# One change to a two-layer transformer kernel: modulation of layer 2 after the linear attention, q and k stored feature-major with three-run gathers, first row maxima ahead of second-half stores

## What is computed

```python
# layer 1, first half: linear attention, 16 heads of 16, rope, elu+1, chunks of 64
# layer 1, second half: gelu MLP, 2048 wide, 4-bit weights with block scales
# layer 2, first half: causal softmax attention, 16 heads of 16, with rope and biases
# layer 2, second half: RMS norm, causal softmax attention without rope,
#                       RMS norm, SwiGLU-like MLP 1024 wide with a low-rank term
x = x + gate * block(layernorm(x) * (1 + scale) + shift)     # each half
att = softmax(q @ k.T / 4, causal) @ v                       # the two softmax attentions
```

## Time and profile before

| what | us |
|---|---|
| median of 3 runs | 708.69 (708.49 to 711.36) |
| profiled execution | 708.0 |
| its span, first to last instruction | 706.1 |
| PE busy | 654.3 (93%) |
| DVE busy | 457.2 (65%) |
| ACT busy | 334.4 (47%) |
| POOL busy | 149.7 (21%) |
| mean granted TensorE clock | 0.988 of full |

### The profile page before, as it was taken

How to read it: one execution, slowest core, us unless ns; L and a number is a source line. 1 busy time by engine, 2 the same in 40 slices (tenths; PEclk the granted TensorE clock), 3 DMA queues, 4 the chain that set the end, 5 groups by cost and what they waited for, 6 DMA issues and landing times.

```text
span 706.1 us, 10697 instructions
## 1 busy us (share of the span) xinstructions
PE 654.3 (93%) x3990; PEld 405.8 (57%) x3990; DVE 457.2 (65%) x970; ACT 334.4 (47%) x531; POOL 149.7 (21%) x194
## 2 busy tenths in 40 slices
PE   4999979999999879899999998897999999999996
PEld 3667647777777656455444434483554444368884
DVE  5668787777777388778888602557788886242223
ACT  5334243333333423345567684561564657843332
POOL 3002224555555601310000000031100001003331
PEclk9999799999999999999999999999999999999999
DMA  7602410000000002663000000037410000050001
GB/s 263 227 0 91 128 44 0 24 23 22 1 0 1 0 1 75 190 186 92 2 2 2 1 2 1 1 125 227 137 54 2 2 2 2 20 160 1 1 0 59
DMA packets 36415, 38.34 MB, mean 54 GB/s; under 512 B 4034, under 2 KB 35292, under 8 KB 36108
## 3 DMA queue, kind: packets, MB, share of 16 engines
q1 hardware_dynamic: 36364, 37.67, 17.0%
HBM read 30.11 MB, written 7.34 MB: 53 GB/s over the span
## 4 chain that ended last, share of the span: by engine, by line
PE 47%; issue 22%; POOL 12%; DVE 11%; ACT 3%; DMA 2%; SPq 2%; POOLq 0%; DVEq 0%; ACTq 0%
POOL it_lo L1602 9%; PE psum L782 9%; PE psum L742 8%; PE psum L768 8%; PE psum L454 4%; DVE m L1285 3%; PE psum L455 3%; PE psum L456 3%; POOL wd L1581 2%; PE psum L771 2%; PE psum L745 2%; PE psum L471 2%; PE psum L570 1%; DVE mx L1285 1%; SPq L345 1%
## 5 line engine op out<-in xcount | busy, mean ns | idle before, releaser
L962 ACT ACTIVATE pt<-psum 128x1024 f32<-128x1024 f32 (+1 forms) x192 | 148.1, 811 | 93.2 <-PE psum L771 65.1
L1285 DVE TENSOR_REDUCE mx<-psum 128x1 f32<-128x512 f32 (+3 forms) x216 | 132.4, 665 | 16.3 <-PE psum L742 8.3
L742 PE MATMUL psum<-kr,qr 96*128 96x512 bf16 (+3 forms) x384 | 108.6, 332 | 5.7 <-DVE m L1285 2.7
L768 PE MATMUL psum<-qr,kr 99*128 99x512 bf16 (+3 forms) x384 | 97.6, 327 | 1.5 <-ACT pt L962 1.3
L1602 POOL TENSOR_TENSOR it_lo<-it,it_hi 128x512 fp32r<-128x512 f32 x48 | 67.3, 1402 | 146.2 <-ACT it_hi L1006 144.6
L782 PE MATMUL psum<-pt,vp 128*32 128x512 f32 (+3 forms) x768 | 81.7, 498 | 0.0
L454 PE MATMUL psum<-h_hi,wf_hi 128*128 128x512 f32 x192 | 75.4, 393 | 1.7 <-issue 1.7
L742 PEld LDWEIGHTS psum<-kr,qr 96*128 96x128 bf16 x384 | 36.3, 98 | 68.0 <-DVE mx L1285 29.4
L1006 ACT CAST it_hi<-it 128x512 fp32r<-128x512 f32 x48 | 29.9, 623 | 95.7 <-DVE it L1360 95.7
L455 PE MATMUL psum<-h_lo,wf_hi 128*128 128x512 f32 x192 | 74.8, 390 | 0.0
L456 PE MATMUL psum<-h_hi,wf_lo 128*128 128x512 f32 x192 | 74.8, 389 | 0.0
(11 more groups left out here) (201 smaller groups left out, 1087.1 us busy)
## 6 DMA issues: line engine op xcount, KB each, us to landing
qr<-parts_scratch SPq DMA_DIRECT2D x48, 128.0 KB, 2.7
kr<-parts_scratch SPq DMA_DIRECT2D x48, 128.0 KB, 2.6
parts_scratch<-parts SPq DMA_DIRECT2D x12, 384.0 KB, 3.2
wmod<-in_L_wmod SPq DMA_DIRECT2D x1, 1536.0 KB, 6.3
parts_scratch<-qr SPq DMA_DIRECT2D x4, 384.0 KB, 3.2
x<-in_L_attn_x SPq DMA_DIRECT2D x2, 512.0 KB, 4.3
wmod<-in_L_wmod SPq DMA_DIRECT2D x1, 1024.0 KB, 5.3
packed<-in_L_ffn_gate_W_packed SPq DMA_DIRECT2D x1, 1024.0 KB, 7.2
```

The lines of the kernel that those rows point to most:

```text
L742: m = pe.matmul(b, qr[0:PARTS_ROWS, c, h, (qt - 4 * c) * P:(qt - 4 * c + 1) * P], kr[0:PARTS_ROWS, ch, h, 0:w], start=True, stop=not diag)
L768: m = pe.matmul(bank[4 + 2 * at[0] + j][:, 0:w], kr[0:PARTS_ROWS + 3, kt // 4, h, (kt % 4) * P:(kt % 4 + 1) * P], qr[0:PARTS_ROWS + 3, c, ...
L962: act.activation(pt[:, n % 4, :, 0:w], psum[:, b:b + 2, 0:w], ACT.Exp, scale=0.25).then_inc(S["ex"], 1)
L1285: dve.tensor_reduce(dst, bank[at[0]][:, 0:k * w].rearrange("p (k w) -> p k w", k=k), AX, ALU.max).then_inc(S["p1_mx"], 1)
```

## The change

It does these things: (1) `wmod1` gets bytes beside `wmod0` and is loaded as soon as layer 1's weights are converted; its twelve calls move behind `update(0)`, eight ahead of layer norm 1's transposes and four behind, each with one filler matmul in front, in place of the fillers of 20 and 8. In the linear attention three fillers per tile stand in their place from tile 1 on. The copy on DVE moves behind `halves(1)`, and PE waits for it ahead of the MLP. (2) The memset of `vp` is cut in four, behind `it_lo` of units 4 to 7 (and behind the scaling in the odd ones). (3) The rows of q and k are reordered to (feature, head) by permuting weights and biases on the host; the pieces are ordered low, middle, high for k and high, middle, low for q, so that one `spread` is 6 DMAs, of 384, 256 and 128 KB for q and for k, each gated by its own store. The order in which the six products are summed changes with it. (4) `row_max(l, 0)` goes ahead of `parts_out(l, 1, 0)` on SP. (5) The six fillers ahead of each attention's first score go.

```diff
-        (wmod0, raw0), (wmod1,), (scale,), (parts, vp), (b_hi, m_hi) = overlay(
+        (wmod0, raw0), (_, wmod1), (scale,), (parts, vp), (b_hi, m_hi) = overlay(
...
-            [("wmod1", [P, KC, 1536], F32)],
+            [("wmod0_", [P, KC, 1536], F32), ("wmod1", [P, KC, 1536], F32)],
...
-        scr = nc.dram_tensor("parts_scratch", [4, P, 3, T], BF16, kind="Internal").ap()
+        scr = nc.dram_tensor("parts_scratch", [4, 3, P, T], BF16, kind="Internal").ap()
...
-            sp.wait_ge(S["mod_mm"], 2)
+            sp.wait_ge(S["wt_hi"], 5)
+            sp.wait_ge(S["wt_lo"], 4)
             load(wmod1[:, :, :], a["L1_wmod"].rearrange("(c p) n -> p c n", p=P), "ld_wmod1")
...
-            sp.wait_ge(S["mod_mm"], 3)
+            sp.wait_ge(S["mod_mm"], 2)
             for j in range(FC[0] // 2):
...
-                    sp.dma_start(scr[w2, :, :, tok], piece(l, w2, half)).then_inc(S[f"pw{2 * half + dt}"], 16)
+                    sp.dma_start(scr[w2, :, :, tok].rearrange("s p t -> p s t"), piece(l, w2, half)).then_inc(S[f"{'qk'[is_k]}w{2 * half + dt}"], 16)
...
-                sp.wait_ge(S[f"pw{2 * half + dt}"], 32 * (l + 1))
-                for is_k, (dst, order) in enumerate([(qr, (0, 1, 0, 1, 0, 2)), (kr, (1, 1, 2, 2, 0, 1))]):
-                    for slot, part in enumerate(order):
-                        sp.dma_start(dst[slot:PARTS_ROWS:6, half, 8 * dt:8 * dt + 8, :],
-                                     scr[2 * dt + is_k, :, part, tok].rearrange("(h d) t -> d h t", d=DH)
+                for is_k, dst in enumerate((qr, kr)):
+                    sp.wait_ge(S[f"{'qk'[is_k]}w{2 * half + dt}"], 16 * (l + 1))
+                    for first, part, n in ((0, 0, 3), (3, is_k, 2), (5, 2 * is_k, 1)):
+                        src = scr[2 * dt + is_k, part:part + n].rearrange("s (d h) t -> (s d) h t", d=DH)
+                        sp.dma_start(dst[DH * first:DH * (first + n), half, 8 * dt:8 * dt + 8, :], src[:, :, tok]
                                      ).then_inc(S[f"qr_ld{2 * half + dt}"], 16)
...
                 spread(l, 0, 1)
+                row_max(l, 0)
                 parts_out(l, 1, 0)
-                row_max(l, 0)
                 parts_out(l, 1, 1)
...
             for t in range(NT):
-                if t >= 2:
-
-                    if t == 2:
-                        pe.wait_ge(S["ld_wmod1"], 16)
-                    modulation(wmod1, 1, 7, 2 * t - 4)
-                    m = modulation(wmod1, 1, 7, 2 * t - 3)
-                    if t == 7:
-                        m.then_inc(S["mod_mm"], 1)
+                if t >= 1:
+                    idle(3, 7)
...
             pe.wait_ge(S["q_e"], 8)
-            pe.wait_ge(S["mod_cp"], 3)
             attention_transposes(0)
...
-            idle(20, 4)
+            pe.wait_ge(S["ld_wmod1"], 16)
+            for j in range(8):
+                idle(1, 4)
+                modulation(wmod1, 1, 5, j)
             layer_norm(1)
-            idle(8, 4)
+            for j in range(8, 12):
+                idle(1, 4)
+                m = modulation(wmod1, 1, 5, j)
+            m.then_inc(S["mod_mm"], 1)
             pe.wait_ge(S["ln_f"], 8)
             pe.wait_ge(S["ln_hl"], 8)
+            pe.wait_ge(S["mod_cp"], 3)
             mlp(0)
...
-                            pe.wait_ge(S[f"qr_ld{2 * c + g // 2}"], 16 * 12 * (l + 1))
+                            pe.wait_ge(S[f"qr_ld{2 * c + g // 2}"], 16 * 6 * (l + 1))
...
                             if blk == 0:
-                                idle(6, 4)
                                 pe.wait_ge(S["kr_ones"], 4)
...
-            modulation_copy(2, 1, 7, 0, 12)
             modulation_rest(0)
...
             halves(1)
+            modulation_copy(2, 1, 5, 0, 12)
             modulation_rest(1)
...
-                    pool.memset(vp[:, :, :, :], 1.0).then_inc(S["vp_ones"], 1)
...
                     if n % 2 == 1 and f == 0 and n // 2 + 2 < FC[f]:
                         scaled(n // 2 + 2)
+                    if f == 0 and 4 <= n < 8:
+                        if n == 4:
+                            pool.wait_ge(S["mod_mm"], 3)
+                        pool.memset(vp[:, 2 * n - 8:2 * n - 6, :, :], 1.0).then_inc(S["vp_ones"], 1)
+                        pool.wait_ge(S["vp_ones"], n - 3)
...
+    spread = _np.arange(D).reshape(2, 8, DH).transpose(0, 2, 1).reshape(-1)
+    for n in ("L1_attn_Wq", "L1_attn_Wk", "L1_ffn_Wq", "L1_ffn_Wk"):
+        given[n] = _np.ascontiguousarray(given[n][:, spread])
```

More of the change, by code:

```diff
@@ L326, in build @@
             att_t at_e wo_m ysem bt x_upd
-            qt sp_h sp_r sp_m sp_l sp_p pw0 pw1 pw2 pw3 qr_ld0 qr_ld1 qr_ld2 qr_ld3 vp_e
+            qt sp_h sp_r sp_m sp_l sp_p qr_ld0 qr_ld1 qr_ld2 qr_ld3 vp_e
             p1_s p1_mx m_max m_step m_t m_c m_ld0 m_ld1 s2 ex pv ob ot at_r
@@ L331, in build @@
             dq w_sc wf_h wf_l g_m u_m gl_s it_s it_h it_l fdn out_done""".split()
+        names += [f"{z}w{i}" for z in "qk" for i in range(4)]
         names += [f"nat{i}" for i in range(FC[1])] + [f"ld_scale{i}" for i in range(4)]
@@ L926, in middle @@
                     half, n = divmod(w, 4)
-                    act.copy(piece(l, n, half)[:, (1, 2)[n % 2], :], rest[:, w % 4, :]
+                    act.copy(piece(l, n, half)[:, 1, :], rest[:, w % 4, :]
                              ).then_inc(S["sp_m"], 1)
@@ L935, in split @@
                             for i in range(4):
-                                act.wait_ge(S[f"pw{i}"], 32)
-                        act.copy(piece(l, n, half)[:, (0, 1)[n % 2], :], bank[w % 4][:, :]
+                                act.wait_ge(S[f"qw{i}"], 16)
+                                act.wait_ge(S[f"kw{i}"], 16)
+                        act.copy(piece(l, n, half)[:, (0, 2)[n % 2], :], bank[w % 4][:, :]
                                  ).then_inc(S["sp_h"], 1)
@@ L1182, in rope_cos @@
                     dve.wait_ge(S["rp_add"], 8 * l + t - 1)
-                dve.tensor_tensor(t1[:, t % 2, :].rearrange("p (h d) -> p h d", d=DH),
-                                  bank[4 + 2 * (t % 2)][:, :].rearrange("p (h d) -> p h d", d=DH),
-                                  rope_c[:, l, t, :].unsqueeze(1).to_broadcast([P, 2 * H, DH]), ALU.mult
-                                  ).then_inc(S["rp_t1"], 1)
+                if l == 0:
+                    z = [v.rearrange("p (h d) -> p h d", d=DH) for v in (t1[:, t % 2, :], bank[4 + 2 * (t % 2)][:, :])]
+                    c = rope_c[:, l, t, :].unsqueeze(1).to_broadcast([P, 2 * H, DH])
+                else:
+                    z = [v.rearrange("p (g d h) -> p g d h", g=4, h=8) for v in (t1[:, t % 2, :], bank[4 + 2 * (t % 2)][:, :])]
+                    c = rope_c[:, l, t, :].unsqueeze(1).unsqueeze(3).to_broadcast([P, 4, DH, 8])
+                dve.tensor_tensor(z[0], z[1], c, ALU.mult).then_inc(S["rp_t1"], 1)
             def rope_sin(l, t):
@@ L1691 @@
             inputs[n].reshape(FC[1], P, KC, P).transpose(0, 3, 2, 1).reshape(F1, D))
[L1692 to L1693 removed]
+    spread = _np.arange(D).reshape(2, 8, DH).transpose(0, 2, 1).reshape(-1)
+    for n in ("L1_attn_Wq", "L1_attn_Wk", "L1_ffn_Wq", "L1_ffn_Wk"):
+        given[n] = _np.ascontiguousarray(given[n][:, spread])
+    given["bias_rows"] = _np.concatenate(
+        [_np.array(inputs[n]) for n in ("L0_attn_bq", "L0_attn_bk", "L0_attn_bv", "L0_attn_bg")]
+        + [_np.array(inputs[n])[spread] for n in ("L1_attn_bq", "L1_attn_bk")])
     for name, arr in [*given.items(), ("rope_cos", cos), ("rope_sin", sin)]:
```

31 lines of the change are left out of this document (16 added, 15 removed).

## The result

The changed kernel takes 719.7 us (median of 4 runs, 717.6 to 722.2); the kernel before took 708.9 beside it. The ratio is 1.0134, 95% interval 1.0104 to 1.0164. It is slower, by 10.8 us by the medians and 9.5 us by the ratio, where 706.2 us, 2.5 us faster, was forecast. The profiled execution took 719.4 us, its span 717.5, against 706.1.

A forecast was written before the change was run, and what follows sets the result against it. PE's waits with DVE close behind bound linear attention, a PE-independent POOL/ACT/DVE loop the MLP, DVE the attention starts; -1.0 + 0.2 + 2.2 - 1.6 - 2.3 = -2.5 us gave 706.2 on the 708.69 median, range 702.5 to 711.5.

The forecast's parts named there:

- Linear attention, -1.0: Linear attention: fillers replace modulation pairs, DVE then limits, w_lo and the add to x come 1.0 us earlier; bounds 0.4, 2.0.
- The clock of 1.00 from 70 to 78 us: Sign in the linear attention: denser fillers keep TensorE at full clock there, with the last w_lo about 1 us earlier.
- Around layer norm 1, +0.2: Behind update 0: the twelve calls hide under DVE's chain; only DVE's 0.16 us copy with its hand-over adds, +0.2 us.
- rival B: Modulation stretch behind update 0: the clock falls there, kernel slower, 708 to 713 us, middle 711; chance 0.22.
- over 6.0: Condition for the clock-fall rival behind update 0: it decides once the eight calls take more than 6.0 us; 5.7 expected.
- Memset, +2.2: MLP loop: odd-unit memsets make it_lo collide with wf_lo, about 1.1 us each; even ones cost 0; bounds 0 and +4.0.
- First attention, -1.6: First attention, ahead of the first score: the six fillers' 1.81 us go, 1.6 us kept because scores may run at half clock.
- gathers half as many in number come earlier than needed and give nothing: First attention: fewer gathers give no gain, since PE reaches the first bank by the splits; 0 us.
- Second attention, -2.3: Second attention: earlier gathers shorten PE's waits, and removed fillers give 1.3 us; sum -2.3, bounds -0.5 and -3.5.
- Half the issues ... bring `qr_ld0` some 4 us forward: Second attention, SP: at 0.74 us per issue, fewer gathers let PE start 0.4 to 0.5 us before 478.14.
- rival D: Gathers: 384 KB pieces land later than three of 128, DMA engines limit, second attention starts as before; 707 us, chance 0.04.
- Rival C: Both attentions: without fillers first scores run longer at half clock, gaining 0.5 each instead of 3.9 together; 709.1 us, chance 0.08.

The follow-up runs named there:

- the repeated change: The changed kernel unaltered, measured again beside its two halves and against the kernel before: 721.7 us, ratio 1.0148.
- the one-column pattern: Gathers half alone, rows two apart, its 28 fillers behind update 0 replaced by 12 fillers, each with two unread one-column matmuls: 708.4 us, repeated 710.7.
- The run with six calls in the gap: Changed kernel with six spaced gather pieces and even-unit memsets; six modulation calls in PE's wait in update 0, then 20 fillers, six calls after layer norm: 710.3 us.
- the second comparison: The gathers half alone with rows two apart, modulation and memset as before, measured again against the kernel before: 707.8 us, ratio 0.9925.

## Why the prediction was wrong

**Linear attention, -1.0.** Right in mechanism, and a little large. From the first `kv_pair` matmul to the add to x, nine profiled executions with the modulation in its old place took 33.6 to 34.1 us in seven cases and 36.9 in two; nine with it moved took 32.7 to 34.0, medians 33.8 and 33.4: 0.4 us, and no execution with the long case. The clock of 1.00 from 70 to 78 us did not come in the first execution: it was 0.84 in 72 to 76 and 0.73 in 76 to 80. Over all runs it mostly did: with the calls in the linear attention the clock was at 1.2 GHz for 6.8 to 17.1 us between 68 and 90 us in all nine profiled executions (17 in the two long ones), with the fillers in their place for 3.4 us in three and not at all in six. DVE sets the pace there, so little of it reached the end, and TensorE waited for the add to x instead.

**Around layer norm 1, +0.2.** The first step that failed: that the twelve calls hide under DVE's chain, at the price of DVE's copy alone. At full clock the eight hide better than I thought, a filler and a call being 0.58 us and not 0.71. But I had charged the stretch for its length alone and given the fall of the clock (rival B) 0.22. It fell in all nine profiled executions with the calls behind update 0, and the stretch took 20.4 to 25.2 us; in the seven without them or their pattern it took 18.3 to 18.4, every time. The copy was too small as well: in the two executions with all twelve calls where the clock was low least (some 3.4 us ahead of the MLP, as long as in three without calls that lost nothing by it) the MLP still began 0.7 us late, waiting for `mod`, and its first it_lo, at 1.2 GHz, came another 1.5 us late. Rival B's mechanism was right in the place and the price (+4.5 in the profiled execution, for 2 to 7), but not in its condition: the eight took 4.7 us, not over 6.0, and it fell all the same; in the repeated change it fell at 90.5 us, and there they took over 8. The forecast put at nothing what rival B names, the longer wait of TensorE ahead of the calls. It was 0.5 us in the kernel before; with the calls behind it, it was 1.6 us in the two executions with a stretch of 20.6 and 20.7 us, 2.1 to 2.4 in three of 22.7 to 22.9, and 3.1 to 3.4 in three where the clock fell already at 90.5 to 92.9 us (a stretch of 22.3 to 25.2 us, one of them with twice the fillers). That the wait decides how early the clock falls is not shown; that it is not needed for a fall is, since the one-column pattern lost the clock behind a wait of 0.5 us.

On the clock, a row stood against "TensorE: Matmul & The Clock Gate" of the Trainium skill (section "What's actually happening"), which lets it drop after idleness. The run with six calls in the gap bears the row out: TensorE had no gap from 81.4 us on and the clock was down at 92.0.

**Memset, +2.2.** Right in place, mechanism and size: +2.0, in the odd units only. By the rule of "GPSIMD Engine Reference" of the Trainium skill (section "Key points") that I weighed against it, the even ones would have added 1.8; beside the operations of DVE, wf_lo's two inputs included, they added nothing. For it_lo beside wf_lo the trace agrees with that rule, 2.00 for 0.99 us.

**First attention, -1.6.** The second step that failed. The removed fillers and the earlier maxima gave 1.65 us, and the sentence behind it failed: "gathers half as many in number come earlier than needed and give nothing". They landed 2.5 to 6 us later each and filled the engines, and the row maxima and stores came late behind them: +4.8 right behind the first score.

**Second attention, -2.3.** From maximum to score 2.9 us were won, but with the first maximum 1.0 later and 3.0 lost behind. The step "Half the issues ... bring `qr_ld0` some 4 us forward" counted SP's time only. What an issue costs in the DMA engines I did not price at all, and rival D, which is just this, got 0.04 and 707 us. This half alone came to +4.0 us by the ratio against -3.9 forecast for both attentions; with the rows spread it came to -3.8, and to -5.3 in the second comparison, around the forecast. Rival C, that without the fillers the first scores give most of the gain back, did not come either.

**The sum.** Of the 13.5 us between 706.2 and 719.7, about 8 are the half with the gathers (-3.9 forecast, +4.0 measured) and the rest is the stretch behind update 0 and the first half's remainder (+7.1 measured for the half, +1.4 forecast). Some 1.4 us of the profiled difference is a clock that fell to 1.2 GHz for 3.4 us between 262 and 270 us in code that the change doesn't touch: that stage took 44.7 us in twelve profiled executions and 46.1 in five, all five with the calls moved. Why the two go together wasn't settled. With the stretch's median (+4.3), the MLP (+2.0) and the linear attention (-0.4) the first half should cost 5.9 us; the last microsecond of its 7.1 stays open. The earlier load of `wmod1`, forecast at nothing, is not in it: from the start to the first `kv_pair` the two groups of nine have medians of 57.0 us (old place) and 56.6.

## What to carry to other kernels

A DMA's price has two parts, its issue and its time in the engines: when a change merges gathers, look at which SBUF rows a piece writes, and spread them, before counting issues. One-column matmuls are not free where TensorE would only wait: moved ahead of the MLP, they came with a fall of the clock in every profiled execution, and the stretch to the MLP's first product was 2 to 7 us longer. And where a wait is shortened by giving its transfer priority, the next transfer in that queue decides, so price it too.

## What the runs showed of the hardware that was not expected

- Gathers of 128 KB onto 16 neighbouring rows ran at 100 to 160 GB/s with the DMA engines full and landed after 8.2 us (k); onto rows six apart the same gathers landed after 2.6 us with the engines at 53%. A 12 KB transfer issued behind the gathers landed after 8.3 us with neighbouring rows, 5.5 with rows two apart and 2.3 with rows six apart. Stores from all 128 rows reached 389 GB/s.
- With rows two apart, 384, 256 and 128 KB pieces landed after 4 to 6 us: better than side by side (5.3 to 8.9), but not like six apart (2.6 to 2.9).
- The clock fell at 92.0 us with TensorE busy without a gap since 81.4, at the end of 2.84 us of one-column matmuls. With fillers alone around layer norm 1, twelve or 28, it fell in three of seven profiled executions (99.0 to 100.6 us) and was back before the MLP; with fillers and one-column matmuls it fell in all eleven, and in nine of them the MLP's first units ran at 1.2 GHz.
- A memset on POOL of 0.96 us beside a two-input operation of DVE lengthened neither; a two-input subtraction on POOL beside the same operation doubled it (0.99 to 2.00 us).
